# Two mixture FFNs around an attention: part of the routing laid between the quarters of the first slots

## The reference, cut to what matters

```
x = x + 0.5 * ffn(layernorm(x))
x = x + attention(layernorm(x))
x = x + 0.5 * ffn(layernorm(x))

ffn(x):
    xln   = ln(x, ln1)
    state = xln @ Ws
    x     = x + (sigmoid(xln @ Wr) * (xln @ Wv)) @ Wo
    h     = ln(x, ln2)
    conf  = sigmoid(h @ conf_w)                       # three experts
    bids  = conf * shares * sigmoid(h @ w_diff) + h @ W_aff
    win   = argmax(bids)
    scale = conf[win] / (conf[win] + 1e-6)
    expert 0, 1: relu(h @ K[e]) ** 2 @ V[e]           # 256 x 1024 x 256
    expert 2:    ((h @ W1) * sigmoid(state @ W2)) @ W3
    return x + expert[win](h) * scale
```

## Time and profile before

| | |
|---|---|
| time, median of 3 runs | 1073.96 us (1073.0 to 1076.77) |
| profiled execution: its time, and its span | 1074.48 us, 1072.8 us |
| TensorE, VectorE, ScalarE, GpSimd busy | 86%, 69%, 55%, 51% of the span |
| first FFN, second FFN | 0 to 446 us; 689 to 1072.8 us |
| mean granted clock of TensorE | 0.934 of full |

### The profile page before, as it was taken

How to read it: one execution, slowest core, us unless ns; L and a number is a source line. 1 busy time by engine, 2 the same in 40 slices (tenths; PEclk the granted TensorE clock), 3 DMA queues, 4 the chain that set the end, 5 groups by cost and what they waited for, 6 DMA issues and landing times.

```text
span 1072.8 us, 20288 instructions
## 1 busy us (share of the span) xinstructions
PE 918.3 (86%) x6490; PEld 847.3 (79%) x6490; DVE 743.2 (69%) x1870; ACT 587.4 (55%) x1279; POOL 544.5 (51%) x656
## 2 busy tenths in 40 slices
PE   7898763899999998788998799888867898999997
PEld 6786653799999998686888688677747898899986
DVE  4639989668866565365776567779997689666653
ACT  3737653554555554245554555677746654555553
POOL 3425755667666666481123000246755767666664
PEclk8968977699999999989999999999998899999999
DMA  7304325456655554220011112302327456455542
GB/s 267 139 1 170 125 99 174 142 170 205 191 165 158 155 153 126 67 88 16 31 60 60 40 30 90 128 20 84 134 119 236 154 172 203 148 159 159 158 138 70
DMA packets 72830, 134.18 MB, mean 125 GB/s; under 512 B 7406, under 2 KB 54382, under 8 KB 72560
## 3 DMA queue, kind: packets, MB, share of 16 engines
q0 software_dynamic: 19232, 73.75, 20.5%
q1 hardware_dynamic: 53488, 59.02, 18.1%
HBM read 89.42 MB, written 44.64 MB: 125 GB/s over the span
## 4 chain that ended last, share of the span: by engine, by line
DVE 19%; PE 16%; issue 9%; POOL 6%; ACT 5%; POOLq 2%; DMA 1%; DVEq 0%; ACTq 0%; SPq 0%
PE bank L430 7%; PE banks4to L1952 3%; PE banks4to L430 2%; DVE state_gate L1442 2%; POOL hr_lo L1628 2%; POOL out_x L1635 2%; POOLq L1663 2%; DVE pT_lo L2242 2%; ACT p L2112 1%; PE bank L1964 1%; DVE chunk_max L2232 1%; POOL attn_x L2340 1%; DVE relu_squared L1444 1%; DVE bn_parts L1335 1%; DVE out_rows L1124 1%
## 5 line engine op out<-in xcount | busy, mean ns | idle before, releaser
L1628 POOL TENSOR_TENSOR hr_lo<-relu_squared,hr_hi 128x512 fp32r<-128x512 f32 (+1 forms) x144 | 178.0, 1251 | 85.1 <-ACT hr_hi L1027 60.5
L430 PE MATMUL bank<-v_hi,hr_hi 128*128 x544 | 159.0, 292 | 27.9 <-POOL hr_lo L1628 25.8
L430 PE MATMUL bank<-v_hi,hr_lo 128*128 x544 | 155.5, 286 | 0.0
L430 PE MATMUL bank<-v_lo,hr_hi 128*128 x544 | 155.5, 286 | 0.0
L1430 DVE TENSOR_TENSOR relu_squared<-relu 128x512 f32<-128x512 f32 (+1 forms) x108 | 102.4, 953 | 62.3 <-ACT relu L1001 38.2
L430 PEld LDWEIGHTS bank<-v_hi,hr_hi 128*128 128x128 f32 x544 | 104.8, 193 | 33.7 <-issue 33.7
L1027 ACT CAST hr_hi<-relu_squared 128x512 fp32r<-128x512 f32 (+1 forms) x36 | 21.5, 597 | 186.9 <-DVE relu_squared L1444 186.9
L430 PEld LDWEIGHTS bank<-v_hi,hr_lo 128*128 128x128 f32 x544 | 104.9, 193 | 0.0
L430 PEld LDWEIGHTS bank<-v_lo,hr_hi 128*128 128x128 f32 x544 | 104.8, 193 | 0.0
L1565 POOL DMA_INDIRECT routed_rows<-out_rows,row_index x64 | 65.0, 1016 | 66.0 <-DVE row_index L1178 51.1
L1421 DVE TENSOR_TENSOR slot_zT_lo<-banks4to,slot_zT_hi 128x512 fp32r<-128x512 f32 (+1 forms) x66 | 40.5, 653 | 81.7 <-ACT slot_zT_hi L985 81.7
(11 more groups left out here) (334 smaller groups left out, 3159.2 us busy)
## 6 DMA issues: line engine op xcount, KB each, us to landing
kx_hi<-first_product_halves POOLq DMA_DIRECT2D x36, 512.0 KB
kx_lo<-first_product_halves POOLq DMA_DIRECT2D x36, 512.0 KB
slot_z<-routed_rows SPq DMA_DIRECT2D x60, 256.0 KB
slot_row<-routed_rows SPq DMA_DIRECT2D x30, 258.0 KB
attn_x<-x_after_ffn SPq DMA_DIRECT2D x16, 256.0 KB, 2.8
attn_out<-x_after_ffn SPq DMA_DIRECT2D x16, 256.0 KB, 2.6
x_after_attention<-attn_out SPq DMA_DIRECT2D x16, 256.0 KB, 2.1
x_rows<-x_after_attention SPq DMA_DIRECT2D x8, 512.0 KB, 4.0
```

Source lines behind the costliest of these rows:

```text
L430: mm = pe.matmul(outv, w(pw), m(pm), start=(n_first and k == 0), stop=(n_last and k == 2))
L1628: pool.tensor_tensor(b.hr[j % 2][1][:, 2 * q:2 * q + 2, 0:m], b.sq[n % 2][:, :, 0:m], b.hr[j % 2][0][:, 2 * q:2 * q + 2, 0:m].bitcast(F32) ...
```

## The change

It moves work between places of the engines' lists; no arithmetic changes.

- **Columns.** setup_slots becomes setup_slots(n), n = 0, 1, 2, with 32, 32 and 16 products, into bank 5 and no longer bank 6, on TensorE after Wo(k) for k = 1, 2, 3. For these k, transpose_z(k + 3) comes ahead of bids(k - 1). VectorE copies each part after stats2(k); bids(g) waits for part g + 1.
- **Last group.** The loops of ffn_a run to k = 6. On TensorE bidT(5), the first half of Wo(7), sT(0), the second half of Wo(7) follow. On VectorE early_slots comes right behind rank(4), ahead of h_lo(5) and x2(6), and stats2(6) behind gv(7), g_lo(7) and residual(6). GpSimd runs k_in(0), rowz(6), k_in(1), rs2(6).
- **Routing in the slots.** The slots now hold the rest of group 5 (prefix, gates, win, rank, z2(6) and scatter(5)) with the routing of groups 6 and 7. In TensorE's list bids(6) and bidT(6) stand on either side of V(0). scatter(6) goes in two halves into slots 3 and 4, scatter(7) into slot 5, pads into slot 6. The late steps move one slot on at most; late_numbers goes behind orow(5).
- **Attention's weights.** Their load goes to slot 8's place in SyncE's list, their five splits to slots 9 to 13 (ScalarE) and 10 to 14 (VectorE), one each. SyncE no longer waits for them ahead of slot 0.
- **Memory.** `pad_rows` shares the place of `wqk_hi` and is loaded at each ffn_b; the second out buffer has a place of its own; slot 0 and group 6 turn in other banks.

The diff, cut to its core:

```diff
-        elif s:
-            pe.wait_ge(s.st_raw, 1)
+        if s and g < 3:
+            pe.wait_ge(s.kb, g + 1)
...
+    def setup_slots(n):
+        if n == 0:
+            pe.wait_ge(s.st_raw, 1)
+        else:
+            pe.wait_ge(f["posr"], n)
+        if n < 2:
+            pe.wait_ge(s.k[n], 32)
             for h in range(HC):
-                raw = b.raw_kx[e][1] if h < HC // 2 else b.raw_k[:, e]
-                column(pe, b.bank(6), e * HC + h, lambda c: raw[:, c], h % (HC // 2) * P, b.ln[:, 3])
-        pe.wait_ge(s.w1, 16)
-        for fc in range(CC):
-            column(pe, b.bank(6), 2 * HC + fc, lambda c: b.raw_w1[:, c], fc * P, b.ln[:, 3])
-        for fc in range(CC):
-            mm = column(pe, b.bank(6), 2 * HC + CC + fc, lambda c: b.raw_sf[:, c], fc * P, b.ln[:, 1])
+                raw = b.raw_kx[n][1] if h < HC // 2 else b.raw_k[:, n]
+                mm = column(pe, b.bank(5), h, lambda c: raw[:, c], h % (HC // 2) * P, b.ln[:, 3])
+        else:
...
-        else:
-            Wo(k)
         if k >= 2:
             r.prefix(k - 2)
         if k:
@@ -648,47 +650,63 @@
         if s and k == 0:
             pe.wait_ge(s.lo, EARLY)
             pe.wait_ge(s.bias, 1)
-        if k + 1 < NG:
-            Wo(k)
+        Wo(k)
+        if s and 1 <= k <= 3:
+            setup_slots(k - 1)
+            transpose_z(pe, b, f, k + 3)
+            r.bids(k - 1)
+            continue
         if k:
             r.bids(k - 1)
         if s and k == 0:
             setup_states()
         if k + 3 < NG:
             transpose_z(pe, b, f, k + 3)
+    r.bidT(last - 2)
+    Wo(last, range(0, 2))
     slot.sT(0, 0)
     slot.sT(0, 1)
+    Wo(last, range(2, GT))
...
     slot.K(0, 0)
+    r.prefix(last - 2)
+    slot.K(0, 1)
     slot.sT(1, 0)
     slot.sT(1, 1)
-    r.bidT(last - 1)
-    slot.K(0, 1)
+    r.T2(last - 1, (0,))
     slot.K(1, 0)
-    r.prefix(last - 1)
+    r.T2(last - 1, (1,))
     slot.K(1, 1)
     slot.sT(2, 0)
     slot.sT(2, 1)
-    r.T2(last, (0,))
+    r.bids(last - 1)
     slot.V(0)
-    r.T2(last, (1,))
+    r.bidT(last - 1)
     slot.K(2, 0)
-    r.bids(last)
     slot.K(2, 1)
     slot.sT(3, 0)
     slot.sT(3, 1)
+    r.prefix(last - 1)
     slot.V(1)
-    r.bidT(last)
+    r.T2(last, (0,))
     slot.K(3, 0)
+    r.T2(last, (1,))
     slot.K(3, 1)
     slot.sT(4, 0)
     slot.sT(4, 1)
+    r.bids(last)
+    slot.V(2)
+    r.bidT(last)
+    slot.K(4, 0)
+    slot.K(4, 1)
+    slot.sT(5, 0)
+    slot.sT(5, 1)
     r.prefix(last)
-    slot.V(2)
-    for j in range(4, NSLOT):
+    slot.V(3)
...
-            pe.wait_ge(f["hlo"], 2 * (NG - 1))
+            pe.wait_ge(f["gv"], 2 * NG)
...
-            if n == 0:
-                pe.wait_ge(f["gv"], 2 * NG - 1)
-            elif n == 1:
-                pe.wait_ge(f["sigr"], 2 * NG)
-            elif n == 2:
-                pe.wait_ge(f["gv"], 2 * NG)
+            if n == 3:
+                pe.wait_ge(f["hlo"], 2 * (NG - 2))
...
     shi(0, 0)
     shi(0, 1)
-    r.bd(last - 1)
+    r.conf(last - 2)
+    r.z2(last - 1, range(GT))
     relu(0, 0)
     square(0, 0)
     relu(0, 1)
+    square(0, 1)
     shi(1, 0)
     shi(1, 1)
-    square(0, 1)
     relu(0, 2)
     sigm(0)
     square(0, 2)
     relu(0, 3)
-    r.conf(last - 1)
-    r.z2(last, range(0, 2))
+    r.h_hi(last - 1, (0,))
     gated(0)
-    r.z2(last, range(2, GT))
     relu(1, 0)
+    relu(1, 1)
+    r.z2(last, range(GT))
     square(1, 0)
-    relu(1, 1)
     square(1, 1)
+    r.h_hi(last - 1, (1,))
     relu(1, 2)
     sigm(1)
     square(1, 2)
     relu(1, 3)
     shi(2, 0)
     shi(2, 1)
-    r.h_hi(last, (0,))
     gated(1)
-    r.h_hi(last, (1,))
+    r.bd(last - 1)
     for j in range(2, NSLOT):
         relu(j, 0)
         square(j, 0)
-        if j == 3:
+        if j == 2:
+            r.conf(last - 1)
+        elif j == 3:
+            r.h_hi(last, (1,))
+        elif j == 4:
             r.conf(last)
         relu(j, 1)
         square(j, 1)
-        if j == 2:
-            r.bd(last)
         relu(j, 2)
         sigm(j)
         square(j, 2)
@@ -1073,6 +1091,13 @@
             shi(j + 1, 0)
             shi(j + 1, 1)
         gated(j)
+        if j == 2:
+            r.h_hi(last, (0,))
+        elif j == 3:
+            r.bd(last)
...
+        if k == KNOWN + 1:
+            r.early_slots()
...
+        x2(k)
+        if k < NG - 2:
             stats2(k)
+        if s and 1 <= k <= 3:
+            dve.wait_ge(s.kb_mm, k)
+            if k < 3:
+                dve.tensor_copy(b.kbias[:, k - 1], b.bank(5)[:, 0:HC]).then_inc(s.kb, 1)
+            else:
+                dve.tensor_copy(b.kbias[:, 2, 0:CC], b.bank(5)[:, 0:CC])
+                dve.tensor_copy(b.sbias[:], b.bank(5)[:, CC:2 * CC]).then_inc(s.kb, 1)
         if s and k in (2, 3):
             split_lo(dve, k_plan(b), 4 * (k - 2), 4 * (k - 1), s.k_hi, s.k_lo)
         if s and k == 5:
             split_lo(dve, trans_plan(b), 0, T_ITEMS, s.t_hi, s.t_lo)
-        if s and k == 6:
-            split_lo(dve, attention_plan(b), 0, A_ITEMS, s.a_hi, s.a_lo)
-        if k - 2 == KNOWN - 1:
-            r.early_slots()
+    gv(NG - 1, 0)
+    gv(NG - 1, 1)
+    g_lo(NG - 1)
+    r.residual(NG - 2)
+    stats2(NG - 2)
...
     slo(0, 0)
     slo(0, 1)
-    r.stats2(last)
+    r.bid_sum(last - 2)
+    r.gates(last - 2)
+    r.x2(last)
     sq(0, 0)
+    r.win(last - 2)
+    r.rank(last - 2)
     sq(0, 1)
     slo(1, 0)
     slo(1, 1)
-    r.bid_sum(last - 1)
+    r.stats2(last)
     sq(0, 2)
     gated(0)
-    r.gates(last - 1)
+    sq(1, 0)
+    r.h_lo(last - 1, (0,))
+    sq(1, 1)
     r.residual(last)
-    sq(1, 0)
-    r.win(last - 1)
-    sq(1, 1)
-    r.rank(last - 1)
     slo(2, 0)
     slo(2, 1)
     sq(1, 2)
     gated(1)
-    r.h_lo(last, (0,))
+    r.h_lo(last - 1, (1,))
     orow(0)
-    r.h_lo(last, (1,))
     for j in range(2, NSLOT):
         sq(j, 0)
-        if j == 3:
+        if j == 2:
+            r.bid_sum(last - 1)
+        elif j == 3:
+            r.h_lo(last, (1,))
+        sq(j, 1)
+        if j == 2:
+            r.gates(last - 1)
+        elif j == 4:
             r.gates(last)
-        sq(j, 1)
-        if j == 4:
+        elif j == 5:
             r.late_places()
-        elif j == 5:
+        elif j == 6:
             r.late_regions()
-        elif j == 6:
-            r.late_numbers()
+            r.late_alone()
         if j + 1 < NSLOT:
             slo(j + 1, 0)
             slo(j + 1, 1)
         sq(j, 2)
         gated(j)
+        if j == 2:
+            r.win(last - 1)
+            r.rank(last - 1)
+        elif j == 4:
+            r.win(last)
+            r.rank(last)
         orow(j - 1)
         if j == 2:
+            r.h_lo(last, (0,))
+        elif j == 3:
             r.bid_sum(last)
-        elif j == 3:
-            r.win(last)
-            r.rank(last)
+        elif j == 4:
             r.late_tiles()
-        elif j == 4:
+        elif j == 5:
             r.late_starts()
-        elif j == 5:
-            r.late_alone()
+        elif j == 6:
+            r.late_numbers()
+        if s and 0 <= j - EARLY_SLOTS - 2 < A_ITEMS:
+            split_lo(dve, attention_plan(b), j - EARLY_SLOTS - 2, j - EARLY_SLOTS - 1, s.a_hi, s.a_lo)
...
+    pool.wait_ge(f["early"], 1)
+    if s:
+        for one in s.stored:
+            pool.wait_ge(one, 32)
+    k_in(0)
+    rowz(NG - 2)
+    k_in(1)
+    rs2(NG - 2)
...
-    tail.rs2(last)
     hrlo(0, 0)
     hrlo(0, 1)
+    tail.scatter(last - 2)
+    tail.rs2(last)
     hrlo(0, 2)
     hrlo(0, 3)
+    tail.k_in(2)
     tail.rowz(last)
-    tail.k_in(2)
-    hrlo(1, 0)
-    hrlo(1, 1)
-    tail.scatter(last - 1)
-    hrlo(1, 2)
-    hrlo(1, 3)
+    for n in range(4):
+        hrlo(1, n)
     pool.drain()
     tail.k_in(3)
     send(0)
     for j in range(2, NSLOT):
         hrlo(j, 0)
         hrlo(j, 1)
-        if j == 4:
+        if j == 3:
+            tail.scatter(last - 1, range(0, 2))
+        elif j == 4:
+            tail.scatter(last - 1, range(2, GT))
+        elif j == 5:
             tail.scatter(last)
-        elif j == 5:
+        elif j == 6:
             tail.pads()
...
+        if s and j + 2 == EARLY_SLOTS:
+            sp.dma_start(b.raw_a[:], w_qkv).then_inc(s.a, 16)
```

More of the change, by code:

```diff
@@ L448, in ffn_a_sync @@
     if s:
-        w1, k_w, v_w, w_qkv = late
+        w1, k_w, v_w = late
         for e in range(2):
@@ L630, in ffn_a_tensor @@
         setup_bids()
-    for k in range(NG):
+    for k in range(last):
         if k >= 2:
             r.bidT(k - 2)
-        if s and k == 2:
-            setup_slots()
         if k == 0:
@@ L939, in ffn_a_scalar @@
     normalize(act, b, f, 2, range(GT))
-    for k in range(NG):
+    for k in range(NG - 1):
         if 0 < k < NG - 2:
@@ L1592, in ffn_a_gpsimd @@
     rs1(2)
-    for k in range(NG):
+    for k in range(NG - 1):
         if k:
             rs2(k - 1)
-        if k == NG - 1:
-            pool.wait_ge(f["early"], 1)
-            if s:
-                for one in s.stored:
```

(4 more changed lines are left out.)

104 lines of the change are left out of this document (53 added, 51 removed).

## The result

The changed kernel takes **1109.11 us** (median of 4 runs, 1108.36 to 1110.17) where the kernel before takes 1074.46 on the same chip (1073.0 to 1076.77): ratio **1.032**, interval 1.030 to 1.034. The forecast was 1077 with a range of 1064 to 1086: 32 us short, and 23 us outside of the range. It lay 2.5 us on the slower side, less than the 3.2 that it called measurable, so it had hardly forecast the direction. The profiled execution has a span of 1106.7 us, 33.9 more than before; the mean granted clock of TensorE fell from 0.934 to 0.913.

What follows compares the result with a forecast made beforehand. GpSimd's loop bounds the slot part, VectorE paces the group part. From 1074.48: +11 + 2.8 - 3.3 - 2.5 - 5.7 - 2.7 - 2.5 = -2.9, so 1077.4, on the median's footing 1077; range 1064 to 1086.

Steps and rivals of the forecast that it cites:

- Columns: First FFN's group part: bias columns in three batches bring VectorE's z_lo(4) earlier; 11 us gained (4 to 14).
- Last group: End of group part: splits and early_slots leave the chain ahead of gv(7); K(0,0) 14.6 and 8.3 us earlier.
- Attention splits: Last group, first FFN: VectorE's splits of attention weights, 5.5 us, leave the chain ahead of gv(7).
- Slots 0 to 2: Routing of groups 5 to 7 lies here; hr_lo(2,0) at +46 from K(0,0), hr_lo(3,0) 18.2 later; net +2.8 and -5.7 us.
- the new wait: TensorE's order puts bids(6) ahead of V(0), so V(0) waits; TensorE idles some 13 us, comes back at half clock.
- Slots 3 to 6: Steps only move one slot on; scatter(6) halves 0.6 each, just-in-time K(4) and gates(7) 2.1: -3.3 and -2.7 us.
- a slack of 8 us: Slot part: a TensorE delay under 8 us is absorbed, one above is not.
- The late flag: Slot 8's rows come later, making V(6) 8 us late plus 2 for half clock; 8 absorbed: -2.5 us per FFN.
- (a): Slots start by GpSimd's chain alone, V(0) not late: 9.5 us per FFN, 1058, or 1068 for half; chance 0.20.
- (b): Bias columns run at half clock in all three batches: gain 4, not 11; 1084; chance 0.15.
- (c): Flag later: late_numbers held by two hr_lo, rows' load meets weight loads; 2.5 to 5 more per FFN, 1082 to 1087; 0.13.
- (d): Slot 0's rows land after the last product; K(0,0) some 3 us later per FFN, 1083; 0.08 with all unnamed.

Runs made afterwards that it cites:

- all orders eased: Changed kernel with every V ahead of its routing step, square ahead of split in slots 2 to 5, V(6) first, slot 8's splits behind: 1091.52 us, ratio 1.014.

## Why the prediction was wrong

- **Columns: mechanism right, a little too small.** +11 forecast; alone they bring K(0,0) 11.5 us earlier and 13.4 in the medians, and in the changed kernel rv(7) starts at 137.46 instead of 151.78, 14.3 earlier. The low end of my gain took off 5.3 us for VectorE's waits on the second and third batch; the second cost 0.3, none is recorded in the third.
- **Attention splits: wrong as a cost.** I took 5.5 us out of the chain by the row's duration. The late splits alone gave none, since 4 of the 4.83 were a hold by v_lo. I had stated the same kind of hold in the paragraph on small operations and did not look whether a removed row was one.
- **Last group: right in the first FFN, too good in the second.** gv(7) is 8.4 us earlier beside the columns' 14.3 (175.75 to 153.08), as forecast, but in part by luck. The hold is gone there for a reason that I did not give: the tables stand ahead of h_lo(5) and are over at 151, before the three v_lo start at 152.26 (the operation that took 4.26 us takes 0.23). In the second FFN it is at 808.12, 802.9 without the shift of 5.2, where I had 800.9: nothing gained. From gv(7) to K(0,0) it is 14.3 and 12.0 instead of 10.4, with a wait of 2.81 and 1.37 for slot 0's rows, which I had called over.
- **Slots 0 to 2 and the new wait: right in mechanism, 2 to 3 us too small.** The idle is 12.92 (13 forecast), hr_lo(2,0) follows K(0,0) by 47.8 and 47.3 (46), hr_lo(3,0) follows by 19.1 and 19.0 (18.2). The kernel before with this wait alone shows its price: 8.5 us per FFN.
- **Slots 3 to 6: the failed step.** I wrote that they "only move one slot on", that scatter(6)'s halves cost 0.6 each, and that the rest is 2.1: 3.3 and 2.7 us, where 10.8 and 11.4 were measured. The halves cost 0.4 and 0.5 together. Slots 3 and 4 lose 8.2 and 7.5 us. There routing steps in TensorE's list (prefix(6), bidT(7), prefix(7)), each with a wait of 1.35 to 3.49 us, and the lower clock of V(1) and V(3) behind them make K late. I judged TensorE by a slack of 8 us, so I did not walk its list through these slots. The slack was 5.4 in a late slot and 0 to 1.7 in slots 2 to 4, and with leads of 4.4 to 6.1 us the changed kernel lacks some 2 to 3.6. The other 2.6 and 3.9 us lie in slots 5 and 6, beside scatter(7) and the pads; no run takes them apart. My own sign for these slots, the first hr_lo of slots 4 and 5 14 to 16 us apart, missed: 17.2.
- **The late flag: too small.** 2.5 us forecast, 5.3 and 4.6 measured from slot 7 on, of which slots 7 and 8 are 4.1 and 3.9. In the first FFN another 1.1 lie in slots 10 to 13, which hold late splits and were put at nothing. Slot 8's rows came 20.4 us behind hr_lo(6,0) (288.13 to 308.54), not 16: asked for at +14.5, not 12.9, and there 5.9 later, not 3 (5.8 in the second FFN, where no attention weights are loaded). Why they are asked for and land later stays open in the main. Further, V(6) was not the only one behind them: the square of slot 7 stands behind slot 8's split on VectorE.
- **Sums.** In the second FFN 811.2 and 46 make 857.2, where I wrote 857.4, and the terms that I list for GpSimd up to rowz make 23.1, not 23.3; neither changes the forecast by more than 0.2 us.
- **Rivals.** (a) is refuted by the 12.92. (b) didn't happen: only half of the first batch ran slowly (3.03 us for 16; 1.84 and 1.93 for others). (c) is right in that the flag and the rows come later; of its reasons the trace shows one meeting of late_numbers with one hr_lo (1.24 us at 297.93). It is small beside slots 3 to 6. (d) is right in part: 2.81 and 1.37 us.

What stays open: with all orders eased, slots 2 and 3 still take 17.5 us. TensorE's waits there (2.2 for the rank, 0.8 for the bids, lower clock in K(2) and K(3)) explain part of it. The waits are released by VectorE and ScalarE, and VectorE was busy for 17.9 of the 18.8 us of slot 5 in the changed kernel, and 16.0 of the 17.0 of slot 4 with all orders eased. How much is VectorE's own load, how much its hold in gates(7), and how much TensorE's order was not tested apart; nor whether a third group's routing can be laid there at all without loss.

## What to carry to other kernels

Before filling a pipeline's idle places, write down for each engine how far it is ahead in the very slots that get the work, and how far it must be: the chain from its step to the first one that the loop's pace needs. A slack read in the steady state need not hold in the slots that start the loop. When a row is to be removed, look whether its time is work: a small operation that is long and ends with another engine's may be a hold, and the next operation then inherits it.

## What the runs showed of the hardware

- A tensor-scalar operation and a copy on VectorE, each with its only array input in SBUF, were held by GpSimd's tensor_tensor: 4.26 us instead of 0.20 for 8 columns, 1.21 instead of 0.17 for a copy of 3 columns. With two array inputs the same was seen: 3.13 us instead of 0.17 for 12 columns.
- Behind 2.51 and 0.65 us of idle TensorE came back at the lower clock: V(1) took 8.5 us at a mean granted clock of 0.64, V(4), behind no wait, 5.8 at 1.00. V(3), behind 3.49 and 0.97 us of idle, took 7.3 at 0.77.
